# A fused two-layer transformer kernel: masks spread over the first feed-forward stage, and another order of loads and stores at the start of the last attention

## The reference

```
x = x + 0.5 * ffn0(layernorm(x))      # 256 -> 1024 -> 256, binarized weights, exact gelu
x = x + local_attention(layernorm(x)) # window 64, plus 64 latents, gated
x = x + 0.5 * ffn0(layernorm(x))
x = x + 0.5 * bit_ffn(layernorm(x))   # 256 -> 256, ternary weights
x = x + rel_attention(layernorm(x))   # 16 heads of 16, relative-position tables
x = x + 0.5 * bit_ffn(layernorm(x))
```

```
attn = q k^T + rpe_k[h, :, clip(j - i)] . q_i + rpe_q[h, :, clip(j - i)] . k_j
p    = softmax(attn)
out  = p v + sum over distances n of (sum of p at distance n) * rpe_v[h, n]
y    = out w_proj^T + b_proj
```

## Time and profile before

| | us |
|---|---|
| median of 3 runs | 2227.58 (2226.09 to 2229.26) |
| the profiled execution | 2228.86 |
| its span (first to last instruction) | 2227.0 |
| PE busy | 1968.0 (88%) |
| DVE busy | 1643.5 (74%) |
| ACT busy | 1222.8 (55%) |
| POOL busy | 496.2 (22%) |

### The profile page before, as it was taken

The page is one execution under the profiler, slowest core; times in us unless marked ns, Lnnn a source line. Parts: engine busy times, 40 slices in busy tenths (PEclk is TensorE's granted clock), DMA queues, the critical chain, the costliest instruction groups (busy, mean ns, idle before and its releaser), DMA issues. The chain is left out here.

```text
span 2227.0 us, 74481 instructions
## 1 busy us (share of the span) xinstructions
PE 1968.0 (88%) x32248; PEld 1258.5 (57%) x32248; DVE 1643.5 (74%) x2668; ACT 1222.8 (55%) x1870; POOL 496.2 (22%) x804
## 2 busy tenths in 40 slices
PE   3997898989888956988779999999999999999985
PEld 2664665657565744568745555555555555555543
DVE  7885565565566878867578888888888888888847
ACT  2882322323137853233237777677776777677754
POOL 3000000000000001000134544444443544345410
PEclk7998998999898977999859999999999999999997
DMA  4000000000000010425574555545554555445312
GB/s 144 1 1 1 21 2 21 2 21 3 21 3 1 1 31 18 147 95 228 171 241 126 130 127 144 144 120 133 144 133 110 134 144 144 127 125 143 95 30 76
DMA packets 273791, 195.11 MB, mean 88 GB/s; under 512 B 206744, under 2 KB 260310, under 8 KB 273210
## 3 DMA queue, kind: packets, MB, share of 16 engines
q1 hardware_dynamic: 262586, 139.27, 24.6%
q0 software_dynamic: 10496, 50.75, 6.0%
q10 hardware_dynamic: 384, 0.33, 0.0%
HBM read 91.69 MB, written 93.88 MB: 83 GB/s over the span
## 5 line engine op out<-in xcount | busy, mean ns | idle before, releaser
L2214 DVE TENSOR_REDUCE a1c_nm<-a1c_S 128x1 f32<-128x1024 f32 x512 | 609.3, 1217 | 83.4 <-PE a1c_S L2301 82.9
L2148 ACT ACTIVATE a1c_PT<-a1c_ST 128x1024 f32<-128x1024 f32 x499 | 509.8, 1022 | 67.6 <-PE a1c_ST L2301 64.7
L2165 ACT ACTIVATE a1c_Pb<-a1c_S,a1c_nm 128x192 f32<-128x192 f32 (+1 forms) x512 | 212.2, 415 | 202.0 <-DVE a1c_nm L2214 201.0
L2087 POOL TENSOR_TENSOR a1c_lt<-a1c_lt 128x256 f32<-128x256 f32 (+5 forms) x448 | 253.9, 567 | 35.4
L2204 DVE COPY a1c_PbT<-a1c_T 96x512 f32<-96x512 f32 x256 | 175.8, 687 | 98.7 <-PE a1c_T L2333 96.3
L2301 PE MATMUL a1c_ST<-a1c_Q,a1c_KR 57*128 57x256 f16 (+2 forms) x1066 | 176.3, 285 | 29.8 <-ACT a1c_PT L2148 19.6
L2301 PE MATMUL a1c_S<-a1c_KL,a1c_Q 54*32 54x512 f16 (+11 forms) x3136 | 193.4, 326 | 0.3
L2301 PE MATMUL a1c_S<-a1c_KR,a1c_Q 54*32 54x512 f16 (+13 forms) x2816 | 181.9, 317 | 12.1 <-DMA a1c_Gx<-a_bias 9.5
L2301 PE MATMUL a1c_S<-a1c_Gx,ident 64*32 64x96 f32 (+2 forms) x4352 | 186.0, 242 | 0.0
L2079 POOL DMA_DIRECT2D a_band<-a1c_Pb x128 | 71.1, 555 | 494.6 <-ACT a1c_Pb L2165 494.6
L1150 POOL PARTITION_ALL_REDUCE b_wall<-b_wsum x2 | 0.8, 404 | 791.4 <-DVE b_wsum L1195 791.4
(11 more groups left out here) (366 smaller groups left out, 3984.7 us busy)
## 6 DMA issues: line engine op xcount, KB each, us to landing
a_band<-a1c_Pb POOLq DMA_DIRECT2D x128, 384.0 KB, 3.5
a_bias<-a1b_G SPq DMA_DIRECT2D x32, 768.0 KB, 9.3
a1c_Gx<-a_bias SPq DMA_DIRECT2D x128, 192.0 KB, 4.3
a1c_Dt<-a_band SPq DMA_DIRECT2D x128, 126.0 KB, 3.3
a1c_Q<-a_qk SPq DMA_DIRECT2D x192, 64.0 KB
a1c_Vw<-a_values SPq DMA_DIRECT2D x64, 102.0 KB, 2.9
a1c_KL<-a_qk SPq DMA_DIRECT2D x96, 64.0 KB
a1c_KR<-a_qk SPq DMA_DIRECT2D x90, 64.0 KB
```

What stands on the lines that cost most here:

```text
L2087: add = lambda o, x, y: nc.gpsimd.tensor_tensor(o, x, y, ALU.add)
L2148: nc.scalar.activation(PT[:, q % 8, :, :], place(q), ACT.Exp).then_inc(s["exp"], 1)
L2165: nc.scalar.activation(Pb[:, band_slot(I, c), w0:w1], SP[:, t % 2, I * P - 32 + w0:I * P - 32 + w1], ACT.Exp, bias=nm[:, t // 16 % 2, col: ...
L2214: nc.vector.tensor_reduce(nm[:, t // 16 % 2, col:col + 1], SP[:, t % 2, :], AX.X, ALU.max, negate=True).then_inc(s["max"], 1)
```

## The change

**Masks.** Each of POOL's constants (each memset, each select, the three on `blk` together) now waits for the semaphore `Y` of the feed-forward stage: the first for 9 finished blocks, every following one for one block more, 37 waits in all, the last for 45 of the 64 blocks.

**Buffers.** `Q`, `KL`, `KR` are split into one tensor for each buffer. Those of group 0 (16 KB per partition) lie over `QH`, `Gx` over `QL`, and those of group 1 behind `Pb`, over low parts of keys and tables that the bias reads until its last sum. So `Gx`'s memset moves ahead of POOL's wait for the bias sums, and constant rows of group 1 move from ACT to SP, behind the last store.

**Order on SP.** Group 0's queries, keys and bias rows are issued ahead of the third unit's store. `shift_rows(0)`, `load_bias(1, 0)` and `diagonals(0)` come ahead of `load_keys(1)`, `load_queries(1, 0)` and the load of `b_proj`.

**Waits.** PE no longer waits for POOL's memsets at the attention's start, but at the first transposes of the band (d = 2).

The diff, without the renamings of `Q`, `KLt` and `KRt` in the loads and products and without the repeated waits of the masks:

```diff
@@ ffn_phase
-                beside.gpsimd(pool)
+                beside.gpsimd(pool, s["Y"])
@@ LocalTables
-    def gpsimd(self, pool):
+    def gpsimd(self, pool, blocks):
 
         nc, s = self.nc, self.s
+        block = Count(blocks, MH)
+
+        def next_block():
+            block.k += 1
+            pool.wait_ge(blocks, block.value())
+
+        next_block()
         nc.gpsimd.memset(self.blk[:, :], 1.0).then_inc(s["zero"], 1)
...
+        next_block()
         nc.gpsimd.memset(self.KE[:, :, 0:WIN], 0.0)
...
@@ rel_attend
-        Q = sb("Q", [P, 2, 2, 4, CW], F16)
-        KLt = sb("KL", [P, 2, 4, CW], F16)
-        KRt = sb("KR", [P, 2, 4, CW], F16)
+        Q0 = sb("Q0", [P, 2, 4, CW], F16)
+        KL0 = sb("KL0", [P, 4, CW], F16)
+        KR0 = sb("KR0", [P, 4, CW], F16)
         Gx = sb("Gx", [P, 4, 9, BW])
         nm = sb("nm", [P, 2, 16])
         Pb = sb("Pb", [P, 4 * TPB, GW])
+        Q1 = sb("Q1", [P, 2, 4, CW], F16)
+        KL1 = sb("KL1", [P, 4, CW], F16)
+        KR1 = sb("KR1", [P, 4, CW], F16)
...
+        def constants(eng, n):
+            for g in range(2):
+                r = 64 * g
+                eng.dma_start(Q[n][r + 48:r + 50, :, :, :].rearrange("r h c t -> r (h c) t"),
+                              bass.AP(CST.tensor, 0, [[CW, 2], [0, 8], [1, CW]])).then_inc(s[f"cst_in{n}"], 16)
...
@@ SP
-            bias.sync(sp)
+            for u in range(bias.NU - 2):
+                bias.store(sp, u)
...
             load_bias(0, 0)
+            bias.store(sp, bias.NU - 2)
             load_queries(0, 1)
             load_bias(0, 1)
             bias.last_out(sp)
-            bias.wait_out(sp, 2)
+            bias.wait_out(sp, bias.NU - 2)
             load_values(0)
             load_windows(0, 0)
-            bias.wait_out(sp, 3)
-            sp.dma_start(bp[:, :], A["b_proj"].partition_broadcast(P)).then_inc(s["bp_in"], 16)
-            load_keys(1)
-            load_queries(1, 0)
+            bias.wait_out(sp, bias.NU - 1)
             load_windows(0, 1)
+            constants(sp, 1)
+            ones(sp, 1)
             shift_rows(0)
             load_bias(1, 0)
             diagonals(0)
+            load_keys(1)
+            load_queries(1, 0)
+            sp.dma_start(bp[:, :], A["b_proj"].partition_broadcast(P)).then_inc(s["bp_in"], 16)
             load_queries(1, 1)
@@ POOL
+            nc.gpsimd.memset(Gx[:, :, 8, :], 0.0).then_inc(s["zero"], 1)
             bias.wait_sums(pool)
-            nc.gpsimd.memset(Gx[:, :, 8, :], 0.0).then_inc(s["zero"], 1)
@@ ACT
-            for g in range(2):
-                r = 64 * g
-                act.dma_start(Q[r + 48:r + 50, :, :, :, :].rearrange("r n h c t -> r (n h c) t"),
-                              bass.AP(CST.tensor, 0, [[CW, 2], [0, 16], [1, CW]])).then_inc(s["cst_in"], 16)
...
+            constants(act, 0)
+            ones(act, 0)
@@ PE, turn_band
+                if e == 0:
+                    pe.wait_ge(s["zero"], 4)
@@ PE, by_key
-                if q == 0:
-                    pe.wait_ge(s["one_in"], 32)
+                if q in (0, 32):
+                    pe.wait_ge(s[f"one_in{q // 32}"], 32)
@@ PE, by_query
+                if t == 32:
+                    pe.wait_ge(s["cst_in1"], 16 * 6)
@@ PE, ahead of the steps
-            pe.wait_ge(s["cst_in"], 16 * 6)
-            pe.wait_ge(s["zero"], 4)
+            pe.wait_ge(s["cst_in0"], 16 * 6)
```

More of the change, by code:

```diff
@@ L1879, in rel_attend @@
         VU = sb("VU", [P, 2, TPB, 4, VW])
+        Q, KLt, KRt = (Q0, Q1), (KL0, KL1), (KR0, KR1)
         Vw = sb("Vw", [BW, TPB, 2, 4, VW])
@@ L1911, in rel_attend, with ones @@
         block = ctx.enter_context(nc.Block())
+        def constants(eng, n):
[3 more added lines that the diff above has]
+                              bass.AP(CST.tensor, 0, [[CW, 2], [0, 8], [1, CW]])).then_inc(s[f"cst_in{n}"], 16)
+                for e, K in enumerate((KLt, KRt)):
+                    eng.dma_start(K[n][r + 50:r + 57, :, :], bass.AP(CST.tensor, 7 * e * CW, [[CW, 7], [0, 4], [1, CW]])
+                                  ).then_inc(s[f"cst_in{n}"], 16)
+        def ones(eng, n):
+            for g in range(2):
+                r = 64 * g
+                eng.dma_start(Q[n][r + 56:r + 57, :, :, :].rearrange("r h c t -> r (h c) t"),
+                              bass.AP(CST.tensor, 0, [[CW, 1], [0, 8], [1, CW]])).then_inc(s[f"one_in{n}"], 16)
         bs = B * S
@@ L1954, in load_keys @@
                         for k, part in enumerate((2, 3, 2)):
-                            sp.dma_start(K[r + HD * k:r + HD * k + HD, n % 2, :, :], features(part, n, CW * g, CW)
+                            sp.dma_start(K[n % 2][r + HD * k:r + HD * k + HD, :, :], features(part, n, CW * g, CW)
                                          ).then_inc(s[f"k_in{n % 2}"], 16)
-                        sp.dma_start(K[r + 48:r + 50, n % 2, :, :],
+                        sp.dma_start(K[n % 2][r + 48:r + 50, :, :],
                                      bass.AP(END.tensor, 64 * bs + (NH * e + 4 * hq) * bs + b * S + CW * g,
@@ L2125, in _ @@
             bias.wait_queries(act)
-            for g in range(2):
-                r = 64 * g
-                act.dma_start(Q[r + 48:r + 50, :, :, :, :].rearrange("r n h c t -> r (n h c) t"),
-                              bass.AP(CST.tensor, 0, [[CW, 2], [0, 16], [1, CW]])).then_inc(s["cst_in"], 16)
-                for e, K in enumerate((KLt, KRt)):
-                    act.dma_start(K[r + 50:r + 57, :, :, :].rearrange("r n c t -> r (n c) t"),
-                                  bass.AP(CST.tensor, 7 * e * CW, [[CW, 7], [0, 8], [1, CW]])).then_inc(s["cst_in"], 16)
-            for g in range(2):
-                r = 64 * g
-                act.dma_start(Q[r + 56:r + 57, :, :, :, :].rearrange("r n h c t -> r (n h c) t"),
-                              bass.AP(CST.tensor, 0, [[CW, 1], [0, 16], [1, CW]])).then_inc(s["one_in"], 16)
+            constants(act, 0)
+            ones(act, 0)
             def probabilities(q):
@@ L2364, in by_key @@
                             at = 64 * g
-                            ins = mm(place(q)[:, g, lo - CW * qh:hi - CW * qh], K[at:at + rows, n % 2, c, P * p:P * p + P],
-                                     Q[at:at + rows, n % 2, qh, c, lo - CW * qh:hi - CW * qh], True, True)
+                            ins = mm(place(q)[:, g, lo - CW * qh:hi - CW * qh], K[n % 2][at:at + rows, c, P * p:P * p + P],
+                                     Q[n % 2][at:at + rows, qh, c, lo - CW * qh:hi - CW * qh], True, True)
                 ins.then_inc(s["ST"], 1)
```

22 lines of the change are left out of this document (14 added, 8 removed).

## The result

The kernel after takes 2216.51 us (median of 5 runs, 2215.94 to 2219.21), the kernel before, timed beside it, 2229.26 (5 runs, 2226.09 to 2233.02). The ratio is 0.9945, 95% interval 0.9935 to 0.9956: 12.3 us less, between 9.8 and 14.5. Forecast were 2215.5, in a range from 2210.5 to 2220.5. The profiled execution took 2216.38 us with a span of 2214.4, against 2228.86 and 2227.0 before, so 12.6 us of span are to be found.

What follows compares the result with a forecast made beforehand. PE's own work bounds the kernel nearly everywhere, so only its idle places yield time: 4.3 us (masks) + 7.8 us (attention's start) = 12.1 us, median from 2227.58 to 2215.5 us, range 2210.5 to 2220.5.

Steps and rivals of the forecast that it cites:

- Masks: First feed-forward stage: moving POOL's masks away from its start wins 5.79 us, less 1.45 for the clock: 4.3 us.
- the wait at 57.10: First feed-forward stage: a wait of 1.25 us, from the slow pair of passes at 54.44, that would go.
- The 1.45 us held back for the clock: First feed-forward stage: products starting earlier run 2.9 us at half clock and lose 1.45 us, if the clock rises when before.
- I take nothing, since most masks are shorter than the slack: First feed-forward stage: masks in their new place beside the blocks cost 0 us, against a slack of 0.91 us.
- its own bound of 1.3: Masks in their new place: at worst 0.26 us lost at each of five pairs of passes, 1.3 us.
- the mean of 0.58 us: Masks in their new place: POOL's work per wait, 21.57 / 37 = 0.58 us, beside 0.34 us of DVE idle per block.
- The sentence that cited the Trainium skill: First feed-forward stage: by its rule the four longest selects (1.17 us) could each stop a low part; gain about 1 us smaller.
- Attention's start: From the bias's end to step 10: first scores 9.5 us earlier, shifted rows issued and step 10 passed 9.6 us earlier.
- DVE's wait ahead of the band copy: Attention's start: DVE's first band copy newly waits 2.4 us for the third store's landing, covered by the later shifted rows.
- the rival of slow constant rows: SP ahead of the shifted rows: constant rows take 9.9 instead of 3.5 us; gain 7.5, 2220.1 us; 8%.
- What is late next: Attention, step 12: PE waits 1.8 us for the diagonals, leaving 7.8 of 9.6 us; group 1's loads stay hidden at step 16.
- The clock, taken at nothing: Attention, steps 10 to 13: full clock by step 10 wins 1.5 us more, a later rise loses as much; 0 taken.

Runs made afterwards that it cites:

- keys_first: The kernel after with b_proj and group 1's 26 loads again ahead of the windows, constants and shifted rows; 2228.48 us, ratio 0.9999 to the kernel before.
- shift_early: The kernel after with the shifted rows issued straight behind the first windows, ahead of the wait for the fourth store; 2215.63 us, ratio 0.9940 to the kernel before.
- attend_only: The kernel after with the masks as they were before; 2223.48 us, ratio 0.9967 to the kernel before.
- masks_hlo: The kernel after with each mask waiting for DVE's low part of its block instead of PE's products; 2218.02 us, ratio 0.9952 to the kernel before.
- masks_split: The kernel after with each of the four selects of later made as two of half the size; 2215.05 us, ratio 0.9942 to the kernel before.
- masks_only: The kernel before with the masks' part of the change alone; 2225.54 us, ratio 0.9982 to the kernel before.

## Why the prediction was right

*Masks, 4.3 us forecast, 3.96 measured.* The sum was right through two errors that cancel. The first products of the second layer came 4.8 us earlier (47.40 for 52.21; forecast 4.54), and the wait at 57.10 went. The 1.45 us held back for the clock were not lost. The term "I take nothing, since most masks are shorter than the slack" was mis-sized: the new place costs 2.3 us, over its own bound of 1.3. What failed in it is the reasoning from the mean of 0.58 us and from one held normalising pass. The four longest selects decide, and they hold the low part itself, for up to 0.97 us, with a normalising pass held for another 0.3 behind it. The sentence that cited the Trainium skill named the mechanism and the four selects, and sized it at 1 us; it was set aside because the row showed two low parts unharmed. That row could not exclude it, as was said there. Other rows of the same trace already showed it. Right behind those low parts DVE's sum of two tiles took 1.63 us, for 1.22 where POOL is idle, beside two selects that took 2.49 us together, for the 1.27 of an earlier pair:

```profile
52.88 1.63 DVE L263 TENSOR_TENSOR x<-x,b2h 128x1024 f32<-128x1024 f32 x1
```

```profile
45.62 1.27 POOL L448 TENSOR_SCALAR_AFFINE_SELECT a_of<-a_of 32x512 bf16<-32x512 bf16 x2
...
52.49 2.49 POOL L448 TENSOR_SCALAR_AFFINE_SELECT a_of<-a_of 32x512 bf16<-32x512 bf16 x2
```

*Attention's start.* First scores 9.5 us earlier: 9.6. The third store 18.5 us to landing: 18.5. The fourth store forecast at 1110.1 (1113.7 less 3.6), measured 1109.89; landed at 1128.6, measured 1129.4. DVE's wait ahead of the band copy: 3.74 us instead of 2.4, since it was ready 0.7 us sooner and the store landed 0.6 later than forecast; covered, as said. Windows and constant rows together forecast at 4.5 us took 4.3 (1129.4 to 1133.7), so the rival of slow constant rows is out: six of them issue in 0.3 us each and two in 0.7 (1.37 together). Shifted rows forecast at 1133.1, issued at 1133.71, and step 10 9.0 us earlier instead of 9.6.

*What is late next.* The diagonals, as forecast, but the wait was 0.67 us, not 1.8: PE came 0.7 later and Dt landed 0.4 earlier. At step 12 8.3 us were won and at step 16 7.7, forecast 7.8. The clock, taken at nothing, stands between the two: the stretch at half clock ends 4.0 us behind step 12 (1152.8), before 2.6 us (1163.2), and PE takes 16.06 us from step 12 to step 16, before 15.49. keys_first and shift_early show both halves of this step: 11.7 us of issues put back cost 12 to 13, and 5.2 us won at step 10 alone are worth nothing at step 12.

*The rest.* To the last value product the attention is 8.6 us shorter, 0.9 more than at step 16. attend_only has the same 8.6 and masks_hlo 8.1, but masks_split, with the same attention, only 1.7, and masks_only, with the attention of the kernel before, is 0.9 longer than that. So the 0.9 us can't be told from what single traces differ by, and no wait was found for it. The same holds for the 0.36 us by which the masks' gain shrank between the first stage and the bias's end (3.96 to 3.60), where traces differ by up to 7.7, and for the 0.4 us of the 12.6 that lie in the last stage. Forecast were 12.1 us. The causes are those of the forecast, and their sizes at the first stage's end and at step 16 bear out 4.3 + 7.8 to half a us; that the medians too agree to 1 us is in part luck.

## What to carry to other kernels

Where several transfers and queues end in one wait, ask what each earlier arrival meets next: of 9.5 us earlier scores at most 3 counted, while the order of 26 issues on the queue behind the wait carried 12. When work of GpSimd is put beside an engine with little slack, look at the longest single instruction that reads SBUF: here the four of them decided, not the mean or the sum, and cutting them in half removed the loss. Keep other stores from running beside a bulk store that later steps wait for: here band stores beside it delayed it by 3.6 us, and behind it by nothing.

## What was not expected of the hardware

GpSimd's first tensor_tensor of the attention stage is preceded by 7.1 to 7.7 us in which nothing is waited for (7.46, 7.54, 7.68, and in the last two kernels 7.10 and 7.30). An earlier one of two elements takes this over, and where the instruction had waited 33 us for a transfer it did not show. Whether it is code that is fetched, no trace here says. The Trainium skill (GPSIMD Engine Reference, "2.1 Instruction dispatch") states about 6 us for the first call of a freshly loaded kernel, which there means a routine of this engine's own code, with no instruction in the profile to show for it. The pauses here are over 1 us longer, and no run shows whether they are that case.
